# The products with V of a batch in two groups of two quads on TensorE, in place of three groups

## The chip, the core and the metric

The kernel runs on one NeuronCore of a Trainium2 chip. The metric is the device time of one execution in microseconds, as the median of several runs; the profile comes from one profiled execution, whose own time stands beside its span below.

## The reference

A block of a transformer: cross-attention over a context with a mask, and a mixture of experts behind it. Cut to what matters here:

```
q = split_heads(layernorm(x) @ Wq.T + bq)      # 16 batches, 112 rows, 16 heads of 16
k = split_heads(ctx @ Wk.T + bk)               # 16 batches, 375 rows
v = split_heads(ctx @ Wv.T + bv)
scores = einsum('bhqd,bhkd->bhqk', q, k) / 4
p = softmax(where(mask == 0, -1e9, scores))
x = x + einsum('bhqk,bhkd->bhqd', p, v) @ Wo.T + bo
# then: layernorm, a router, the top 2 of 8 experts for each row, x = x + their weighted sum
```

## The kernel before

Everything is float32 or a split of a float32 number into two parts (a high and a low one), so that a projection is three products. The 16 batches are worked on one after the other in a software pipeline. The function turn(b) of TensorE (L1653 to L1712) writes out by hand the order of the pipeline's turn b, for b = 0 to 14. In a turn TensorE does four things for four different batches, and VectorE (DVE) and ScalarE (ACT) run their own turns, also in an order written out by hand; the engines meet only through semaphores. Nothing is reordered by a scheduler: each engine takes its instructions in the order of the code.

The names that are used from here on, all of them for TensorE work in turn b:

- **H0 to H15** (L1539, heads): scores of one head of the next batch, b+1, 112 x 376, one matmul each. They are only for the row maxima: DVE reads each of them from its bank of PSUM (L1053, "neg_max") to find the maximum. There are two banks for 16 heads, so head s waits until DVE has read head s-2.
- **V0, V2, V1** (values): the values of batch b+1, six matmuls each at L1478.
- **K00, K01, K10, K11** (keys): the keys of batch b+3, in four parts of three matmuls at L1478. In turns 13 and 14 there is no such batch; the output projections of finished rows stand in place of K01 and K11 (12 matmuls each), and K00 and K10 are empty.
- **S0 to S3** (L1554, scores): scores of batch b for softmax, transposed, with mask and maxima folded in; one quad (four heads) each, six matmuls into three banks of PSUM. ACT takes the exponential of a quad in one instruction, L815, here exp0 to exp3, and writes it to one of two buffers ("probs"). All four quads use the same three banks, so each S waits for the exp of the quad before it.
- **O0 to O3** (L1568, outputs): the products with V of the quad. Four heads stand side by side in strips of 32 columns of the array (a tile_position at L1570), 12 matmuls and 12 weight loads of 32 columns, which the profile shows as 24 of each. O(j) waits for exp(j); exp(j+2) waits for O(j), since it writes the same buffer.
- **OT**, **AT** (L1581, L1593): transposes of the finished attention rows of batch b-1. ACT reads AT (L808), then DVE (L1044, "attn_low").
- **MT** (L1544): the transpose of the 16 maxima of batch b+1, at the end of the turn, into the bank that the even heads use. DVE reads it in two instructions (L1062, L1064, here "max_rows") and two DMAs carry it to the operand of the next turn's S0.

Before a turn's first head, H0, TensorE waits for max_rows of the turn before, since H0 overwrites MT's bank; before H1 it waits for attn_low, since H1 overwrites AT's bank:

```
if s >= 2:
    pe.wait_ge(max_read, H * b.n + s - 1)
elif s == 0 and not early(b, 1):
    pe.wait_ge(mx_ready, 2 * b.n)
elif s == 1 and not early(b, 3):
    pe.wait_ge(tl_ready, KD * (b.n - 2))
```

DVE's own order in a turn is: the maxima of H0 to H10, a normalisation, the maxima of H11 to H13, the keys of K01, the maxima of H14 and H15, the keys of K11, max_rows, attn_low. In turn 14 the statistics of finished rows stand ahead of its first maximum. ACT's order around the four exps is: two casts, a copy of the outputs, a copy of values, exp0, a copy of values, exp1, exp2, the two instructions on AT, exp3.

After turn 14 the code for the last batch follows (L1871 on), which begins with O2 and O3 of batch 14, and then the router, a plan of the experts' steps, and the experts' steps.

Of the kernel before, what the change touches and what calls it, by code (L numbers as in the profile page):

```python
# [105 lines left out]
def xattn_moe_kernel(nc, x_rows, x_tiles, ctx_t, mask, wq_t, wk_t, wv_t, wo_t, bq, bk, bv, bo,  # L106
                     router_w, w1, w2, out):
    ctx = ExitStack()
    with ctx:
# [281 lines left out]
        def has(b):  # L391

            return not isinstance(b.n, int) or 0 <= b.n < B
# [1080 lines left out]
        def _(pe):  # L1474
# [6 lines left out]
            def project_keys(b, t, halves=range(KD)):  # L1481
                home = ctx_home(b.n)
                if 0 not in halves:
                    pass
                elif t == 0:
                    pe.wait_ge(ch_ready, b.n + 1)
                    pe.wait_ge(cl_ready, b.n + 1)

                    if early(b, 4):
                        if b.n:  # L1490
                            pe.wait_ge(*{1: (vx_ready, 2), 2: (kf_ready, 4), 3: (vx_ready, 4)}[b.n])
                    else:
                        pe.wait_ge(vx_ready, 2 * (b.n - 1))
                elif not early(b, 4):
                    pe.wait_ge(an_ready, b.n - 3)
                m = slice(t * P, (t + 1) * P)
                terms = [(w[:, 0, k, m], c[home][:, k, :]) for k in halves for w, c in ((wh, ch), (wl, ch), (wh, cl))]
                last = product(ps[:, BK_KV + t, 0:CP], terms, first=0 in halves, final=KD - 1 in halves)
                if KD - 1 in halves:
                    last.then_inc(kproj_done, 1)  # L1500

            def project_values(b, k3):

                if early(b, 1):
                    pe.wait_ge(kf_ready, 2)
                elif k3 == 0:
                    if has(b.after(1)):
                        pe.wait_ge(kf_ready, 2 * b.n + 3)
                    else:
                        pe.wait_ge(resid_added, 1)  # L1510
                elif k3 == 2:
                    if has(b.after(1)):
                        pe.wait_ge(kf_ready, 2 * b.n + 4)
                    else:
                        pe.wait_ge(resid_added, 2)
                m = slice(k3 * CT, (k3 + 1) * CT)
                last = product(ps[0:CT, BK_KV + k3 // 2, D * (k3 % 2):D * (k3 % 2) + D],
                               [(c[ctx_home(b.n)][:, k, m], w[:, 2, k, :]) for k in range(KD)
                                for w, c in ((wh, ch), (wh, cl), (wl, ch))])
                if k3 != 0:  # L1520
                    last.then_inc(vproj_done, 1)
# [3 lines left out]
            def head_scores(b, turns):  # L1525

                for s in turns:
                    if s == 0:
                        pe.wait_ge(q_stacked[b.ring], 48 * (b.lap + 1))
                        pe.wait_ge(k_stacked[b.ring], 96 * (b.lap + 1))  # L1530
# [7 lines that stand above are left out]
                    a, q = s % 2, s // 2  # L1538
                    pe.matmul(ps[0:S, BK_MAX + a, 0:CP], qs[b.ring][0:R_MAX, q, S * a:S * (a + 1)],  # L1539
                              ks[b.ring][0:R_MAX, q, :], start=True, stop=True).then_inc(smax_done, 1)  # L1540

            def max_transpose(b):
                pe.wait_ge(max_read, H * (b.n + 1))
                pe.transpose(ps[0:H, BK_MAX, 0:S], neg_max[:, :], ident[0:S, 0:S]).then_inc(maxt_done, 1)  # L1544

            def quad_scores(b, j):

                if j == 0:
                    pe.wait_ge(mx_stacked[b.ring], 32 * (b.lap + 1))
                if not (early(b, 1) and j < 1):  # L1550
                    pe.wait_ge(pf_ready, QUADS * b.n + j)
                for k3 in range(KT):
                    for q in range(2):
                        last = pe.matmul(ps[0:CT, BK_ST + k3, 2 * S * q:2 * S * (q + 1)],  # L1554
                                         ks[b.ring][0:ROWS, 2 * j + q, k3 * CT:(k3 + 1) * CT],
                                         qs[b.ring][0:ROWS, 2 * j + q, :], start=True, stop=True)
                last.then_inc(st_done, 1)

            def quad_outputs(b, j):

                pe.wait_ge(pf_ready, QUADS * b.n + j + 1)
                if j == 0:
                    pe.wait_ge(vx_ready, 2 * (b.n + 1))
                    if not early(b, 1):
                        pe.wait_ge(ot_ready, b.n)
                for k3 in range(KT):
                    for i in range(4):
                        last = pe.matmul(ps[VC * i:VC * (i + 1), BK_OUT, S * j:S * (j + 1)],  # L1568
                                         vx[b.par][:, k3, 2 * j + i // 2 + HALF * (i % 2), :], pf[j % 2][:, k3, S * i:S * (i + 1)],
                                         start=k3 == 0, stop=k3 == KT - 1, tile_position=(0, VC * i))  # L1570
                last.then_inc(pv_done, 1)

            def out_transpose(b):
                pe.wait_ge(ot_ready, b.n + 1)

                if has(b.after(2)):
                    pe.wait_ge(vx_ready, 2 * b.n + 5)
                else:
                    pe.wait_ge(resid_added, 4 if has(b.after(1)) else 6)
                for j in range(QUADS):  # L1580
                    last = pe.transpose(ps[0:S, BK_KV + 1, P * j:P * (j + 1)], ot[:, S * j:S * (j + 1)], ident[:, :])  # L1581
                last.then_inc(ott_done, 1)
# [70 lines left out]
            def turn(b):  # L1653

                after, before = b.after(1), b.after(-1)

                def heads(*numbers):
                    if has(after):
                        head_scores(after, numbers)

                def scores(j):
                    if has(b):
                        quad_scores(b, j)

                def outputs(of, j):
                    if has(of):
                        quad_outputs(of, j)

                def values(k3):
                    if has(after):  # L1670
                        project_values(after, k3)

                def keys(t, *halves):
                    if has(b.after(3)):
                        project_keys(b.after(3), t, halves)
                    elif halves[-1] == KD - 1:
                        project_output(2 * (b.n - B + 3) + t)

                outputs(before, 2)
                heads(0)  # L1680
                values(0)
                heads(1, 2)
                outputs(before, 3)
                heads(3)
                values(2)
                heads(4, 5)
                scores(0)
                heads(6)
                if has(before):
                    out_transpose(before)  # L1690
                heads(7)
                values(1)
                heads(8, 9)
                scores(1)
                heads(10)
                outputs(b, 0)
                heads(11)
                keys(0, 0)
                heads(12)
                scores(2)  # L1700
                heads(13)
                keys(0, 1)
                heads(14)
                keys(1, 0)
                heads(15)
                keys(1, 1)
                scores(3)
                if has(after):
                    max_transpose(after)
                if has(before):  # L1710
                    attn_transpose(before)
                outputs(b, 1)  # L1712

            first = Batch(0, 0)

# [46 lines left out]
            for b in range(B - 1):  # L1762
                turn(Batch(0, b))
# [108 lines left out]
            before = last.after(-1)  # L1872
# [92 lines left out]
```

## Time and profile before

| what | value |
|---|---|
| time, median of 3 runs | 485.5 us (484.94 to 486.68) |
| time of the profiled execution | 485.71 us |
| span in the profile of that execution | 483.9 us |
| mean granted TensorE clock | 0.929 of full speed |
| busy: TensorE matmul, VectorE, ScalarE | 417.6, 346.5, 268.5 us |

In the profile's rows a time is in microseconds from the start of the span, and the second number is how long the row lasted. "PE" is TensorE's matmuls, "PEld" its weight loads. Matmuls overlap: each row shows a matmul from its start to the end of its way through the array, so the distance from one start to the next is what it costs. A matmul whose weight load could not be hidden shows a row that is some 0.09 us longer than others of its kind (0.43 against 0.34 us for a head, 0.91 against 0.81 us for a quad of scores), because the row then begins with the load. Where starts are subtracted below, such a row counts from 0.09 or 0.10 us later, and that is called its effective start.

### The profile page before, as it was taken

What the parts mean: (1) busy time and instruction counts of PE and PEld (TensorE: products, weight loads), DVE (VectorE), ACT (ScalarE), POOL (GpSimd) and SP (SyncE); (2) the same over time, 40 slices, a digit from 0 to 9 for tenths busy, and PEclk for the clock granted to TensorE, in tenths of its full rate; (3) what the DMA queues carried; (4) which work ended last, traced back from release to release, by engine and by line L of the source; (5) the groups of instructions that cost most, each with busy time, mean ns of one, the idle gap of its engine ahead of it and who ended that gap; (6) DMA issues with size and microseconds to landing.
All of it is one profiled execution on the core that took longest, in us unless ns stands there. A gap on an engine that the chain in (4) does not pass through costs nothing.

```text
span 483.9 us, 10747 instructions
## 1 busy us (share of the span) xinstructions
PE 417.6 (86%) x4187; PEld 387.0 (80%) x4187; DVE 346.5 (72%) x711; ACT 268.5 (55%) x351; POOL 227.4 (47%) x255
## 2 busy tenths in 40 slices
PE   1584669999999999999999999677999999999820
PEld 1472559999999999999999888577999999999820
DVE  2685557787788887787878868874787777767536
ACT  3322225666666556666655464515887888888600
POOL 7263334422322343332220365647477888875430
PEclk9796878999999999999999999659999999999975
DMA  7868947766768887866745027943122322332159
GB/s 170 214 158 180 285 159 160 160 130 145 163 150 163 155 183 152 177 146 135 147 94 108 2 91 260 364 143 93 56 87 78 88 88 88 88 87 78 45 195 303
DMA packets 60227, 69.83 MB, mean 144 GB/s; under 512 B 19185, under 2 KB 55298, under 8 KB 60178
## 3 DMA queue, kind: packets, MB, share of 16 engines
q1 hardware_dynamic: 54242, 56.30, 48.3%
q0 software_dynamic: 4032, 11.02, 7.7%
q10 hardware_dynamic: 1904, 1.84, 1.1%
q8 instruction: 33, 0.54, 0.5%
q14 instruction: 16, 0.13, 0.1%
HBM read 35.64 MB, written 14.78 MB: 104 GB/s over the span
## 4 chain that ended last, share of the span: by engine, by line
PE 73%; DVE 10%; issue 6%; DMA 5%; ACT 2%; POOL 2%; SPq 0%; POOLq 0%; DVEq 0%; ACTq 0%
PE ps L1478 37%; PE ps L1539 12%; PE ps L1554 9%; PE ps L1568 8%; PE ps L1833 2%; PE ps L1581 1%; DVE x_rows_sb L1100 1%; DVE neg_max L1053 1%; DMA y_rows<-y_out,slot_of_row 1%; DMA y_back<-y_rows 1%; DMA rows<-xn_rows,token_of_row 1%; DVE stats L1089 1%; POOL rows L746 1%; DMA keep<-keep_scratch 1%; DMA q_stack<-max_rows 1%
## 5 line engine op out<-in xcount | busy, mean ns | idle before, releaser
L1053 DVE TENSOR_REDUCE neg_max<-ps 112x1 f32<-112x376 f32 x256 | 133.7, 546 | 38.5 <-PE ps L1539 33.7
L815 ACT ACTIVATE probs<-ps 125x1344 f32<-125x1344 f32 x64 | 82.8, 1293 | 43.3 <-PE ps L1554 38.1
L1539 PE MATMUL ps<-k_stack,q_stack 98*112 98x376 f32 x256 | 88.7, 381 | 10.2 <-issue 5.9
L587 POOL TENSOR_TENSOR k_lo<-k_f,k_hi 128x752 fp32r<-128x752 f32 x16 | 28.9, 1804 | 121.9 <-ACT k_hi L789 119.5
L1539 PEld LDWEIGHTS ps<-k_stack,q_stack 98*112 98x112 f32 x256 | 45.7, 181 | 23.6 <-DVE neg_max L1053 13.7
L746 POOL DMA_INDIRECT rows<-xn_rows,token_of_row x42 | 55.2, 1315 | 19.0 <-issue 12.5
L754 POOL DMA_INDIRECT y_rows<-y_out,slot_of_row x42 | 46.4, 1104 | 27.5 <-ACT y_out L985 16.5
L1554 PE MATMUL ps<-q_stack,k_stack 100*125 100x224 f32 x384 | 53.3, 275 | 0.2 <-DMA q_stack<-max_rows 0.2
L1554 PEld LDWEIGHTS ps<-q_stack,k_stack 100*125 100x125 f32 x384 | 51.2, 191 | 1.1 <-ACT probs L815 0.5
L1478 PE MATMUL ps<-w_hi,h_hi 128*128 128x256 f32 x168 | 48.6, 289 | 1.6 <-issue 1.6
L1478 PE MATMUL ps<-flat_t_hi,w_hi 128*128 128x256 f32 x168 | 47.6, 283 | 1.3 <-DVE flat_t_lo L1365 1.3
L1478 PE MATMUL ps<-flat_t_hi,w_lo 128*128 128x256 f32 x168 | 47.3, 282 | 0.0
L1478 PE MATMUL ps<-flat_t_lo,w_hi 128*128 128x256 f32 x168 | 47.3, 282 | 0.0
L1478 PE MATMUL ps<-w_hi,h_lo 128*128 128x256 f32 x168 | 47.0, 280 | 0.0
L1568 PE MATMUL ps<-probs,v_wide 125*32 125x112 f32 x1536 | 47.0, 262 | 0.0
L1478 PE MATMUL ps<-w_lo,h_hi 128*128 128x256 f32 x168 | 46.9, 279 | 0.0
L1568 PEld LDWEIGHTS ps<-probs,v_wide 125*32 125x32 f32 x1536 | 35.1, 109 | 8.0 <-issue 5.6
L966 ACT ACTIVATE h_f<-ps 128x1024 f32<-128x1024 f32 x21 | 21.5, 1026 | 25.2 <-PE ps L1478 25.2
L1478 PEld LDWEIGHTS ps<-flat_t_hi,w_hi 128*128 128x128 f32 x168 | 32.1, 191 | 1.7 <-DVE flat_t_lo L1365 1.7
L1478 PEld LDWEIGHTS ps<-w_hi,h_hi 128*128 128x128 f32 x168 | 31.9, 190 | 2.0 <-issue 1.8
L1387 DVE TENSOR_TENSOR h_lo<-h_f,h_hi 128x1024 fp32r<-128x1024 f32 x21 | 25.7, 1225 | 10.1 <-ACT h_hi L971 10.1
L1478 PE MATMUL ps<-ctx_hi,attn_w_hi 128*128 128x376 f32 x64 | 23.2, 363 | 10.5 <-POOL ctx_lo L578 9.7
(202 smaller groups left out, 1032.4 us busy)
## 6 DMA issues: line engine op xcount, KB each, us to landing
k_stack<-k_hi SPq DMA_DIRECT2D x64, 188.0 KB, 4.5
w_all<-w SPq DMA_DIRECT2D x2, 4096.0 KB, 18.2
k_stack<-k_lo SPq DMA_DIRECT2D x32, 188.0 KB, 5.5
ctx_raw<-ctx_t SPq DMA_DIRECT2D x32, 187.5 KB, 5.4
q_stack<-q_scratch SPq DMA_DIRECT2D x32, 168.0 KB
q_scratch<-q_hi SPq DMA_DIRECT2D x16, 224.0 KB, 3.0
y_back<-y_rows SPq DMA_DIRECT2D x14, 256.0 KB, 4.5
q_scratch<-q_lo SPq DMA_DIRECT2D x8, 224.0 KB, 2.9
```

The lines of the kernel that those rows point to most:

```text
L587: pool.tensor_tensor(kl[:, :, :], kf[:, :, :], kh[:, :, :].bitcast(F32), ALU.subtract)\
L746: pool.indirect_dma_start(rows[t.ring][:, a, :], None, xn_rows, row_of(token_i, t, a))\
L754: pool.indirect_dma_start(y_rows, row_of(slot_i, t, a), yo[t.par][:, a, :], None)\
L815: act.activation(pf[j % 2][:, :, :], ps[0:CT, BK_ST:BK_ST + KT, 0:4 * S], ACT.Exp).then_inc(pf_ready, 1)
L966: act.activation(hf[t.par][:, :, :], silu_source(t), ACT.Silu).then_inc(hf_ready, 1)
L1053: dve.tensor_reduce(neg_max[:, s:s + 1], ps[0:S, BK_MAX + s % 2, 0:CP], AX.X, ALU.max, negate=True).then_inc(max_read, 1)
L1387: dve.tensor_tensor(hl[t.par][:, :, :], hf[t.par][:, :, :], hh[t.par][:, :, :].bitcast(F32), ALU.subtract).then_inc(hl_ready, 1)
L1478: last = pe.matmul(o, lhs, rhs, start=first and n == 0, stop=final and n == len(terms) - 1)
L1539: pe.matmul(ps[0:S, BK_MAX + a, 0:CP], qs[b.ring][0:R_MAX, q, S * a:S * (a + 1)], ks[b.ring][0:R_MAX, q, :], start=True, stop=True).then_i ...
L1554: last = pe.matmul(ps[0:CT, BK_ST + k3, 2 * S * q:2 * S * (q + 1)], ks[b.ring][0:ROWS, 2 * j + q, k3 * CT:(k3 + 1) * CT], qs[b.ring][0:ROW ...
L1568: last = pe.matmul(ps[VC * i:VC * (i + 1), BK_OUT, S * j:S * (j + 1)], vx[b.par][:, k3, 2 * j + i // 2 + HALF * (i % 2), :], pf[j % 2][:, ...
L1833: last = pe.transpose(ps[:, BK_T + t.par, TG * k + P * a:TG * k + P * (a + 1)], rows[t.ring][:, a, k * P:(k + 1) * P], ident[:, :])
```

## The change

The four quads of outputs that are done in a turn stood in three places: O2 of the batch before at the turn's start, right behind O1 at the end of the turn before (one group of two), O3 behind H2, and O0 between H10 and H11. Now O2 stands beside O3 behind H2, and O0 and O1 stand together behind S2. The same instructions are issued, in another order, on TensorE alone.

```diff
@@ -1676,10 +1676,10 @@
-                outputs(before, 2)
                 heads(0)
                 values(0)
                 heads(1, 2)
+                outputs(before, 2)
                 outputs(before, 3)
                 heads(3)
                 values(2)
@@ -1692,12 +1692,12 @@
                 values(1)
                 heads(8, 9)
                 scores(1)
-                heads(10)
-                outputs(b, 0)
-                heads(11)
+                heads(10, 11)
                 keys(0, 0)
                 heads(12)
                 scores(2)
+                outputs(b, 0)
+                outputs(b, 1)
                 heads(13)
                 keys(0, 1)
                 heads(14)
@@ -1709,7 +1709,6 @@
                     max_transpose(after)
                 if has(before):
                     attn_transpose(before)
-                outputs(b, 1)
```

TensorE's instructions across the boundary between two turns, before: MT, AT, O1 and O2 (x12 each), H0, the six matmuls of V0, then H1 and H2.

```order
L1544 MATMUL ps<-ident,neg_max 16x112
L1593 MATMUL ps<-ident,attn_rows 128x112 x2
L1568 MATMUL ps<-probs_97,v_wide_94 32x112 x12
L1568 MATMUL ps<-probs_96,v_wide_94 32x112 x12
L1539 MATMUL ps<-k_stack_90,q_stack_92 112x376
L1478 MATMUL ps<-attn_w_hi,ctx_hi_115 125x256
L1478 MATMUL ps<-attn_w_hi,ctx_lo_116 125x256
L1478 MATMUL ps<-attn_w_lo,ctx_hi_115 125x256
L1478 MATMUL ps<-attn_w_hi,ctx_hi_115 125x256
L1478 MATMUL ps<-attn_w_hi,ctx_lo_116 125x256
L1478 MATMUL ps<-attn_w_lo,ctx_hi_115 125x256
L1539 MATMUL ps<-k_stack_90,q_stack_92 112x376 x2
```

The same boundary on TensorE now; O2 and O3 follow after H1 and H2.

```order
L1544 MATMUL ps<-ident,neg_max 16x112
L1593 MATMUL ps<-ident,attn_rows 128x112 x2
L1539 MATMUL ps<-k_stack_90,q_stack_92 112x376
L1478 MATMUL ps<-attn_w_hi,ctx_hi_115 125x256
L1478 MATMUL ps<-attn_w_hi,ctx_lo_116 125x256
L1478 MATMUL ps<-attn_w_lo,ctx_hi_115 125x256
L1478 MATMUL ps<-attn_w_hi,ctx_hi_115 125x256
L1478 MATMUL ps<-attn_w_hi,ctx_lo_116 125x256
L1478 MATMUL ps<-attn_w_lo,ctx_hi_115 125x256
L1539 MATMUL ps<-k_stack_90,q_stack_92 112x376 x2
L1568 MATMUL ps<-probs_96,v_wide_94 32x112 x12
L1568 MATMUL ps<-probs_97,v_wide_94 32x112 x12
```

Between MT with AT and H0 two quads of outputs have gone; nothing stands there now.

The middle of a turn on TensorE before, from S1: H10, O0, H11, K00 (three matmuls), H12, S2, H13.

```order
L1554 MATMUL ps<-q_stack_93,k_stack_91 125x224 x6
L1539 MATMUL ps<-k_stack_113,q_stack_114 112x376
L1568 MATMUL ps<-probs_96,v_wide_94 32x112 x12
L1539 MATMUL ps<-k_stack_113,q_stack_114 112x376
L1478 MATMUL ps<-ctx_hi_84,attn_w_hi 128x376
L1478 MATMUL ps<-ctx_hi_84,attn_w_lo 128x376
L1478 MATMUL ps<-ctx_lo_86,attn_w_hi 128x376
L1539 MATMUL ps<-k_stack_113,q_stack_114 112x376
L1554 MATMUL ps<-q_stack_93,k_stack_91 125x224 x6
L1539 MATMUL ps<-k_stack_113,q_stack_114 112x376
```

The same stretch of TensorE now, from S1: H10 and H11 in one row, K00, H12, S2, O0, O1, H13.

```order
L1554 MATMUL ps<-q_stack_93,k_stack_91 125x224 x6
L1539 MATMUL ps<-k_stack_113,q_stack_114 112x376 x2
L1478 MATMUL ps<-ctx_hi_84,attn_w_hi 128x376
L1478 MATMUL ps<-ctx_hi_84,attn_w_lo 128x376
L1478 MATMUL ps<-ctx_lo_86,attn_w_hi 128x376
L1539 MATMUL ps<-k_stack_113,q_stack_114 112x376
L1554 MATMUL ps<-q_stack_93,k_stack_91 125x224 x6
L1568 MATMUL ps<-probs_96,v_wide_94 32x112 x12
L1568 MATMUL ps<-probs_97,v_wide_94 32x112 x12
L1539 MATMUL ps<-k_stack_113,q_stack_114 112x376
```

Between S1 and S2 a quad of outputs has gone, and behind S2 two have come.

## Rows read from the trace of the kernel before

**Rows 1.** The page, part 4: the chain that ended last, share by engine.

```profile
PE 73%; DVE 10%; issue 6%; DMA 5%; ACT 2%; POOL 2%; SPq 0%; POOLq 0%; DVEq 0%; ACTq 0%
```

**Rows 2.** Waits of PE's matmuls, 66 to 280 us: total, times, longest.

```profile
PE ps L1539 <- DVE neg_max L1053: 2.3, 2, 1.9
```

**Rows 3.** Windows: stretch, its length, busy of engines, granted clock (PEclk), DMA share.

```profile
65.00:79.00 14.00, 11.92 (x54) 11.10 (x54) 7.43 (x17) 5.64 (x8) 7.88 (x11) 0.70 0.57 158
...
208.00:222.00 14.00, 14.00 (x177) 12.75 (x175) 11.30 (x26) 8.62 (x11) 4.82 (x3) 1.00 0.66 141
```

**Rows 4.** Timeline of PE (start, length, line): MT ending turns 1 and 12.

```profile
97.86 0.26 PE L1544 MATMUL ps<-ident,neg_max 112*16 112x112 f32 x1
...
249.07 0.26 PE L1544 MATMUL ps<-ident,neg_max 112*16 112x112 f32 x1
```

**Rows 5.** Timeline of PE, one boundary: MT, O1+O2, H0, H1+H2, O3, H3.

```profile
207.90 0.26 PE L1544 MATMUL ps<-ident,neg_max 112*16 112x112 f32 x1
...
208.28 1.36 PE L1568 MATMUL ps<-probs,v_wide 125*32 125x112 f32 x48
...
209.56 0.43 PE L1539 MATMUL ps<-k_stack,q_stack 98*112 98x376 f32 x1
...
210.54 0.51 PE L1539 MATMUL ps<-k_stack,q_stack 98*112 98x376 f32 x2
...
210.99 0.78 PE L1568 MATMUL ps<-probs,v_wide 125*32 125x112 f32 x24
...
211.70 0.43 PE L1539 MATMUL ps<-k_stack,q_stack 98*112 98x376 f32 x1
```

**Rows 6.** Timeline of DVE and ACT there: max_rows, attn_low, exp3, maximum of H0.

```profile
208.49 0.26 DVE L1064 TENSOR_TENSOR max_rows<-ps,max_rows 16x112 fp32r<-16x112 f32 x1
209.02 0.58 DVE L1044 SCALAR_TENSOR_TENSOR attn_t_lo<-ps,bv_c,attn_t_hi 128x112 fp32r<-128x112 f32 x2 [0.27 <-ACT attn_t_hi L808]
209.19 1.29 ACT L815 ACTIVATE probs<-ps 125x1344 f32<-125x1344 f32 x1 [0.20 <-PE ps L1568]
...
210.03 0.55 DVE L1053 TENSOR_REDUCE neg_max<-ps 112x1 f32<-112x376 f32 x1 [0.43 <-PE ps L1539]
```

**Rows 7.** Timeline of PE, the middle of that turn: O0, S2, H13.

```profile
202.84 0.78 PE L1568 MATMUL ps<-probs,v_wide 125*32 125x112 f32 x24
...
204.50 0.82 PE L1554 MATMUL ps<-q_stack,k_stack 100*125 100x224 f32 x6
...
205.16 0.34 PE L1539 MATMUL ps<-k_stack,q_stack 98*112 98x376 f32 x1
```

**Rows 8.** Timeline of DVE and ACT there: maxima of H8 to H10, exp1.

```profile
201.88 1.62 DVE L1053 TENSOR_REDUCE neg_max<-ps 112x1 f32<-112x376 f32 x3 [0.33 <-PE ps L1539]
...
202.72 1.29 ACT L815 ACTIVATE probs<-ps 125x1344 f32<-125x1344 f32 x1 [0.43 <-PE ps L1554]
```

**Rows 9.** Timeline of ACT and PE in turn 13: exp1, S2, H13.

```profile
257.64 1.29 ACT L815 ACTIVATE probs<-ps 125x1344 f32<-125x1344 f32 x1 [0.42 <-PE ps L1554]
...
258.98 0.91 PE L1554 MATMUL ps<-q_stack,k_stack 100*125 100x224 f32 x6
259.74 0.33 PE L1539 MATMUL ps<-k_stack,q_stack 98*112 98x376 f32 x1
```

**Rows 10.** Timeline, turn 14's start: exp3, maxima of H0 to H2, H2, O3.

```profile
265.06 1.29 ACT L815 ACTIVATE probs<-ps 125x1344 f32<-125x1344 f32 x1 [0.20 <-PE ps L1568]
...
266.53 1.61 DVE L1053 TENSOR_REDUCE neg_max<-ps 112x1 f32<-112x376 f32 x3
...
267.13 0.42 PE L1539 MATMUL ps<-k_stack,q_stack 98*112 98x376 f32 x1 [0.38 <-DVE neg_max L1053]
267.48 0.78 PE L1568 MATMUL ps<-probs,v_wide 125*32 125x112 f32 x24
```

**Rows 11.** Timeline of PE behind turn 14: S0 of the last batch, O3.

```profile
283.04 0.92 PE L1554 MATMUL ps<-q_stack,k_stack 100*125 100x224 f32 x6 [0.21 <-DMA q_stack<-max_rows]
283.88 0.78 PE L1568 MATMUL ps<-probs,v_wide 125*32 125x112 f32 x24
```

## The prediction, made before the changed kernel ran

> **What bounds the kernel now.** I read the chain of work that ended last first: 73% of it is PE, 10% DVE [rows 1]. So the question is whether PE has gaps in the stretch that changes, the 15 turns. It has nearly none: the list of waits shows 2.3 us for heads that waited for DVE's maxima, in two cases [rows 2], and the window of a whole turn shows PE's matmuls busy for 14.00 of 14 us while DVE has 11.30 and ACT 8.62, with the granted clock at 1.00 [rows 3]. The turns are alike: MT starts at 97.86 at the end of turn 1 and at 249.07 at the end of turn 12, eleven turns of 13.75 us [rows 4]. A turn of DVE is thus 81% full, and every one of its 16 maxima is tied to a head on PE by two banks. PE is full because the order by hand puts other work wherever a head or a quad of scores would have to wait. The change takes such work out of two places, so I ask at each what would then be late.
>
> **What the change saves.** Nothing is computed less. A group of outputs costs something on the way in and on the way out. Way in: H2 starts 0.17 us after H1 (210.71), and O3 at 210.99, 0.28 us after H2 where a head takes 0.17: 0.11 us [rows 5]. The quad's 24 weight loads fill 0.54 us of the row; from O3's start to H3's effective start (211.79) it is 0.80, so 0.26 us on the way out [rows 5]. That is 0.37 us for a group. Over the turns 44 groups become 30 (behind turn 14, O2 keeps a group of its own), so 14 x 0.37 = 5.2 us, if nothing is late next. The row shows this cost; beside it, the Trainium skill (TensorEngine Tiling (Array Packing), Tiling Modes, Key Properties) says that a change of tiling mode drains the array, which speaks for the change, and the trace agrees with its 0.11 and 0.26 us.
>
> **What is late next, first place: the middle of a turn.** S2 needs exp1, and exp1 needs S1. Before, O0 lay between S1 and S2 and hid part of that exp. exp1 runs from 202.72 to 204.01, while S2 started at 204.50 [rows 7, 8], so before it waited for nothing. How soon S2 can follow an exp is seen in turn 13, where it did wait: exp1 ended at 258.93, S2's effective start is 259.08, a release of 0.15 us [rows 9]. With O0 gone from there, S2 can start at 204.01 + 0.15 = 204.16, 0.34 us earlier than before, not the 0.91 us (0.37 of the group and 0.54 of its loads) that left. The heads are not later than that: the maximum of H9 ends two thirds into the row of three, at 202.96, of H10 at 203.50 [rows 8]; with a release of 0.14 us (next part) H11 starts at 203.10, three matmuls of K00 of 0.17 bring H12 to 203.78, S2 could start at 203.95. ACT decides.
> Behind S2 now stand two quads. From the effective start of a quad of scores to the outputs behind it: 283.15 to 283.88, 0.73 us [rows 11]. From the start of a double group to the effective start of the head behind it: 208.28 to 209.65, 1.37 us [rows 5]. So H13 comes at 204.16 + 0.73 + 1.37 = 206.26, where it was 205.16: **1.10 us later**. From H13 on the order is the same to MT. exp2 now waits for O0 too, whose row would run from 204.89 to 205.67; with 1.29 us it is over by 207.0, and S3, which waits for it, stands right ahead of MT, now at 209.0: hidden. I take 1.10 for turns 0 to 12, 14.3 us. In turns 13 and 14 K00 is empty and S2 waited for exp1 already [rows 9]; its start stays, and H13 comes 0.73 + 1.37 - 0.66 = 1.44 us later, 2.9 us for the two.
>
> **Second place: the boundary of two turns.** Before, MT to H3 took 207.90 to 211.79, 3.89 us, with three quads in it [rows 5]; now it has two. H0 needs max_rows, which ended at 208.75 [rows 6], 0.9 us before H0's effective start of 209.65; O1 and O2 covered it. They are gone. The release from DVE to PE is seen where a head did wait: the first of three maxima ended at 266.53 + 0.54 = 267.07, H2's effective start was 267.21, 0.14 us [rows 10]. So H0 starts at 208.89, where it could have followed AT at about 208.28. H1 follows 0.89 us behind, as before, at 209.78; attn_low, which it needs too, ends at 209.60 [rows 6], with its release at 209.74: just hidden, and 0.1 us dearer if V0 ran faster. DVE reads H0 when attn_low is over, 209.60, for 0.55 us, ending between 210.06 (such rows overlap by up to 0.09) and 210.15; H2 starts at 210.20 to 210.29, where 0.17 behind H1 would be 209.95. I take 210.22. O2 begins 0.28 later at 210.50, H3 at 210.50 + 1.37 = 211.87: **0.1 us later** than before, though a quad less was done. O3 needs exp3, which before ended at 210.48 [rows 6] and cannot be later now; O3's turn is at 211.06: hidden. Twelve boundaries at 0.1 give 1.2 us; the one behind turn 0 has no attn_low, I take 0. In front of H2 of turn 14 DVE decides already (it waited 0.38 us) [rows 10]; its start stays, two quads follow in place of one, 1.37 - 0.80 = 0.57 us.
> This rests on V0 and O2 not passing H0 while it waits. In turn 14 exp3 was over at 266.35, and O3 still started only after H2 had waited until 267.13 [rows 10]. That is a rule against this change in the Trainium skill (TensorE: Matmul & The Clock Gate, Part 3, what overlaps and what doesn't): matmuls start and end in program order, only weight loads are pulled ahead; the trace agrees, and if it didn't, H0's wait would be filled.
>
> **The end.** Behind turn 14, O1 no longer stands ahead of S0 of the last batch. S0 waited there for the DMA of max_rows (0.21 us) [rows 11], so the missing 0.57 us come back as a longer wait: 0. DVE, ACT, POOL and the DMA queues get the same instructions in the same order, and longer turns give the loads more room. All that follows hangs on the attention's last rows, so the delay goes through to the end.
>
> **The sum.** 14.3 + 2.9 + 1.2 + 0.6 = 19.0 us on the profiled execution's 485.7 (span 483.9 and 1.8 around it); that execution is 0.2 above the median, so 485.5 + 19.0 = 504.5 us. Read as parts of a turn: 0.37 us saved, some 1.5 us of new waits. Bounds: the release behind an exp or a maximum between 0 (as if hidden) and twice what the rows show moves S2, H0 and H2 by 0.15 each, at most some 0.3 us a turn, 4.5 us over 15 turns; the way into a double group behind S2 between the 0.73 us of rows 11 and 0.1 more adds 1.5 above; the end between 0 and the -0.57 that its cover is worth. That makes 499 to 510.5.
>
> **The rivals.**
> *Fewer groups, waits hidden*: the 5.2 us saved come through, 480.3 us, faster. For it: PE is full, DVE and ACT have 2.7 and 5.4 us to spare in the 14 us. It decides on whether the new waits stay under 0.37 us a turn. Against it: H0 alone waits about 0.6 us for max_rows, whose rows lie on a chain through DVE that nothing shortens. 4%; exactly cancelled, 485.5 us, 2%.
> *Only one place costs*: if H0 hardly waits (max_rows done earlier, since DVE's keys end earlier against MT), the boundary gains about 0.6 us a turn instead of losing 0.1, 13 x 0.7 = 9 us less: 495 us. Against it: from H13 to MT the order is unchanged on every engine, so max_rows should end 0.85 us behind MT's start as before [rows 5, 6]. 10%.
> *The clock*: the stretch from 65 to 79 us shows a granted clock of 0.70 with PE busy for only 11.92 of 14 us, among the waits of 1.9 us for DVE [rows 2, 3]. If waits that are now some 1.5 us of a 15 us turn cost one tenth of the clock over the loop, PE's 13.5 us become 15.0, 1.5 us for 15 turns, 22 us more: 527 us. Between, 511 to 527, if it strikes a part of the turns. Against it: in the rows the clock is at 1.00 in turns with waits of 0.38 us, and the longest new one is about 0.6. The Trainium skill (TensorE: Matmul & The Clock Gate, Part 1) says that an idle array falls to half its clock; no row here shows it for gaps this short. 7%.
> *The forecast*, new waits in both places: 77%.
>
> **How the numbers follow.** The forecast's 504.5 is the likeliest. About 0.3% is what a measurement of this kernel can tell from no change, so faster is 0.04, within 0.3% 0.02, slower 0.94. For 8 in 10, the forecast's bounds and the near part of the two neighbours: 498 to 510.5.
>
> **What would show it.** Right: MT to MT near 15.0 us instead of 13.75; H13 some 2.1 us behind S2's start; PE idle before H0 ended by max_rows, before H2 ended by a maximum, before S2 ended by exp1; 29 double groups and no single ones before the end of turn 14; the same busy time of DVE and ACT over a longer span. Wrong: a turn of 13.4 us with H0 right behind AT (then the waits are hidden), a turn near 14.3 us with an idle time before S2 alone (one place), or a granted clock under 1.00 between 85 and 280 us.

## The result: 503.75 us, slower by 3.9%

The changed kernel takes 503.75 us (median of 4 runs, 502.56 to 505.8) against 485.48 us for the kernel before (4 runs); the ratio is 1.0386, with a 95% interval of 1.0349 to 1.0422. The forecast was 504.5 us, in a range of 498 to 510.5. The profiled execution, the slowest of the four, took 505.8 us with a span of 504.0.

The profile page's chain of work that ended last, by engine, beside [rows 1]; then the list of waits of PE's matmuls and of its weight loads, of 66 to 300 us (total, times, longest), beside [rows 2]; then two lines of the same list for the kernel before:

```profile
PE 66%; DVE 16%; issue 6%; DMA 5%; ACT 3%; POOL 2%; SPq 1%; POOLq 0%; DVEq 0%; ACTq 0%
```

```profile
PE ps L1539 <- DVE max_rows L1064: 7.9, 14, 0.7
PE ps L1539 <- DVE neg_max L1053: 3.7, 4, 2.3
...
PEld ps L1554 <- ACT probs L815: 5.1, 15, 0.4
PEld ps L1568 <- issue: 2.5, 14, 0.2
```

```profile
PEld ps L1568 <- issue: 5.6, 31, 0.2
...
PEld ps L1554 <- ACT probs L815: 0.5, 2, 0.2
```

PE's share of the chain fell from 73% to 66%, DVE's rose from 10% to 16%. One wait is new in the list of matmuls: 14 times before H0 for max_rows, 0.56 us each. Among the weight loads the wait of S2 for exp1, which stood there twice before (turns 13 and 14), now stands there 15 times, 0.34 us each. The idle time on the way into a group of outputs, 5.6 us in 31 places before, is 2.5 us in 14. This list is not a count of groups: PE's timeline has 29 double groups up to the end of turn 14, as forecast, and only those behind H2 show such an idle time. So there are fewer groups, and PE now waits where the quads stood. A whole turn in a window (stretch, length, busy of PE, PEld, DVE, ACT, POOL, granted clock, DMA) and the MTs at the ends of turns 1 and 12, beside [rows 3, 4]:

```profile
219.00:233.00 14.00, 13.41 (x168) 11.74 (x168) 9.95 (x23) 8.58 (x11) 4.82 (x3) 1.00 0.67 141
```

```profile
99.84 0.26 PE L1544 MATMUL ps<-ident,neg_max 112*16 112x112 f32 x1
...
263.82 0.26 PE L1544 MATMUL ps<-ident,neg_max 112*16 112x112 f32 x1
```

PE is busy for 13.41 of 14 us in place of 14.00, at the full clock. Eleven turns take 163.98 us, 14.91 us each where it was 13.75: 1.16 us more a turn.

The boundary of two turns, timeline of PE and of DVE (start, length): MT, H0, H1 and H2, O2 and O3, H3; then max_rows, attn_low, the maximum of H0; beside [rows 5, 6]:

```profile
219.15 0.26 PE L1544 MATMUL ps<-ident,neg_max 112*16 112x112 f32 x1
...
220.15 0.40 PE L1539 MATMUL ps<-k_stack,q_stack 98*112 98x376 f32 x1 [0.55 <-DVE max_rows L1064]
...
221.10 0.68 PE L1539 MATMUL ps<-k_stack,q_stack 98*112 98x376 f32 x2
...
221.71 1.36 PE L1568 MATMUL ps<-probs,v_wide 125*32 125x112 f32 x48
...
223.00 0.42 PE L1539 MATMUL ps<-k_stack,q_stack 98*112 98x376 f32 x1
```

```profile
219.75 0.26 DVE L1064 TENSOR_TENSOR max_rows<-ps,max_rows 16x112 fp32r<-16x112 f32 x1
...
220.28 0.58 DVE L1044 SCALAR_TENSOR_TENSOR attn_t_lo<-ps,bv_c,attn_t_hi 128x112 fp32r<-128x112 f32 x2 [0.27 <-ACT attn_t_hi L808]
...
220.77 0.54 DVE L1053 TENSOR_REDUCE neg_max<-ps 112x1 f32<-112x376 f32 x1
```

H0's effective start is 220.21 (its row is 0.06 us longer than the plain 0.34), 1.06 us after MT, behind max_rows, which ended at 220.01. H3's effective start is 223.08, 3.93 us behind MT: as long as before (3.89 us) with two quads in it in place of three.

The middle of the next turn, the same way: exp1 on ACT, then PE's S2, O0 and O1, and H13; beside [rows 7, 8]:

```profile
227.75 1.29 ACT L815 ACTIVATE probs<-ps 125x1344 f32<-125x1344 f32 x1 [0.42 <-PE ps L1554]
...
229.10 0.91 PE L1554 MATMUL ps<-q_stack,k_stack 100*125 100x224 f32 x6
...
229.94 1.36 PE L1568 MATMUL ps<-probs,v_wide 125*32 125x112 f32 x48
...
231.23 0.43 PE L1539 MATMUL ps<-k_stack,q_stack 98*112 98x376 f32 x1
```

exp1 ends at 229.04, S2's effective start is 229.20, H13 follows at 231.32. From H3 to the next MT (234.07) it is now 10.99 us, where it was 9.83 (211.79 to 221.62): 1.16 us more with one quad more.

### The profile page after: what moved, and what is told of

It reads as the page before. It is cut to its first block, busy times and chain, and to the rows that moved or that the text cites. A ratio compares the mean times of both kernels' runs of the same rounds, so it can differ in the third digit from the quotient of the medians.

```text
span 504.0 us, 10747 instructions
## 1 busy us (share of the span) xinstructions
PE 428.4 (85%) x4187; PEld 390.4 (77%) x4187; DVE 344.3 (68%) x711; ACT 268.0 (53%) x351; POOL 227.5 (45%) x255
## 4 chain that ended last, share of the span: by engine, by line
PE 66%; DVE 16%; issue 6%; DMA 5%; ACT 3%; POOL 2%; SPq 1%; POOLq 0%; DVEq 0%; ACTq 0%
PE ps L1478 33%; PE ps L1539 11%; PE ps L1568 8%; PE ps L1554 8%; DVE neg_max L1053 4%; DVE k_f L1037 3%; PE ps L1832 2%; PE ps L1581 1%; DMA y_back<-y_rows 1%; DMA y_rows<-y_out,slot_of_row 1%; DVE x_rows_sb L1100 1%; DMA rows<-xn_rows,token_of_row 1%; ACT probs L815 1%; DVE max_rows L1064 1%; DVE max_rows L1062 1%
## 5 line engine op out<-in xcount | busy, mean ns | idle before, releaser
L1539 PE MATMUL ps<-k_stack,q_stack 98*112 98x376 f32 x256 | 92.7, 392 | 19.6 <-DVE max_rows L1064 7.9
L1554 PE MATMUL ps<-q_stack,k_stack 100*125 100x224 f32 x384 | 54.6, 278 | 0.8 <-DMA q_stack<-max_rows 0.4
L1568 PE MATMUL ps<-probs,v_wide 125*32 125x112 f32 x1536 | 44.1, 261 | 0.0
L1478 PEld LDWEIGHTS ps<-flat_t_hi,w_lo 128*128 128x128 f32 x168 | 32.7, 194 | 0.0
## 6 DMA issues: line engine op xcount, KB each, us to landing
w_all<-w SPq DMA_DIRECT2D x2, 4096.0 KB, 18.3
```

What stands on the lines that cost most here:

```text
L1478: last = pe.matmul(o, lhs, rhs, start=first and n == 0, stop=final and n == len(terms) - 1)
```

## Experiments

Two theories stood against each other. **Two separate waits**: in the middle O0 was the cover of exp1, at the boundary O1 and O2 were the cover of max_rows and attn_low, and the groups saved are worth less than that. **Only one of the places costs**, or only the number of groups counts. Seven kernels take the change apart, and the changed kernel ran once more beside three of them. In the table a turn is the distance of the MTs at the ends of turns 1 and 12, divided by 11.

| run | median, us | of the kernel before beside it | ratio, 95% interval | a turn, us |
|---|---|---|---|---|
| before | 485.5 | | | 13.75 |
| after | 503.75 | 485.48 | 1.0386 (1.0349 to 1.0422) | 14.91 |
| again | 503.13 | 485.23 | 1.0369 (1.0334 to 1.0403) | 14.91 |
| mid | 495.64 | 485.2 | 1.0237 (1.0184 to 1.029) | 14.35 |
| o0 | 493.7 | 485.2 | 1.019 (1.0141 to 1.0238) | 14.30 |
| bnd | 487.08 | 485.2 | 1.0042 (1.0014 to 1.0069) | 13.82 |
| split | 490.01 | 485.2 | 1.0095 (1.0045 to 1.0145) | 14.09 |
| v0 | 504.2 | 485.23 | 1.0362 (1.0316 to 1.0408) | 14.90 |
| ahead | 498.29 | 485.23 | 1.0269 (1.023 to 1.0307) | 14.66 |
| ahead2 | 497.04 | 485.23 | 1.0223 (1.0155 to 1.0291) | 14.36 |

**One quad alone (o0).** From the kernel before:

```diff
-                heads(10)
-                outputs(b, 0)
-                heads(11)
+                heads(10, 11)
                 keys(0, 0)
                 heads(12)
                 scores(2)
+                outputs(b, 0)
```

> One quad alone is moved: O0 from between H10 and H11 to behind S2, the rest as before. As many groups as before. The theory: S2 then waits for exp1 uncovered; from S2's effective start to H13 0.73 + 0.80 us, so H13 comes at 204.16 + 1.53 = 205.69 in place of 205.16 in the turn of the trace, 0.53 us later in 13 turns and 0.87 us in two: 485.5 + 8.6 = 494.1 us, with PE waiting 0.3 us before S2 for exp1 and 0.3 us before H11 for a maximum. If the order in the middle is indifferent as long as the groups are as many: 485.5 us.

493.7 us, 0.55 us more a turn. The timeline of PE in its middle, S2, O0, H13:

```profile
220.74 0.91 PE L1554 MATMUL ps<-q_stack,k_stack 100*125 100x224 f32 x6
...
221.58 0.78 PE L1568 MATMUL ps<-probs,v_wide 125*32 125x112 f32 x24
...
222.30 0.42 PE L1539 MATMUL ps<-k_stack,q_stack 98*112 98x376 f32 x1
```

S2's row is 0.91 us long, as it is after a wait, and H13 follows S2's effective start (220.84) by 1.54 us; 1.53 was expected. No quad has crossed a boundary and no group was added or lost: this is the price of taking O0 from between S1 and S2. O0 covered two waits there, that of S2 for exp1 and that of H11 for DVE's maximum of H9; ahead and ahead2 below tell them apart.

**The middle alone (mid).** As o0, and O1 follows O0 behind S2 instead of standing at the turn's end; O2 stays at the turn's start.

> The change in the middle of a turn alone: O0 and O1 stand together behind S2, O2 stays at the turn's start, O3 behind H2. As many groups of outputs as before (44). The theory of two separate waits: S2 is bound by exp1, H13 comes 1.10 us later in turns 0 to 12 and 1.44 us in turns 13 and 14 (17.2 us); at the boundary O2 alone still covers max_rows, so the boundary is about 0.47 us shorter by O1 that has left it, 13 times (6.1 us): 485.5 + 11.1 = 496.6 us. If only the number of groups counted: 485.5 us. If the boundary were what costs: near 485 to 487 us.

495.64 us, 0.60 us more a turn (0.63 by the terms of the expectation). Timeline of PE at a boundary: MT, O2, H0, H3.

```profile
212.72 0.26 PE L1544 MATMUL ps<-ident,neg_max 112*16 112x112 f32 x1
...
213.11 0.78 PE L1568 MATMUL ps<-probs,v_wide 125*32 125x112 f32 x24
213.82 0.43 PE L1539 MATMUL ps<-k_stack,q_stack 98*112 98x376 f32 x1
...
216.00 0.42 PE L1539 MATMUL ps<-k_stack,q_stack 98*112 98x376 f32 x1
```

O2 alone covers max_rows: H0 starts right behind it, and MT to H3 is 3.36 us, 0.53 less than before.

**The boundary alone (bnd).** From the kernel before; O1 stays at the turn's end:

```diff
-                outputs(before, 2)
                 heads(0)
                 values(0)
                 heads(1, 2)
+                outputs(before, 2)
                 outputs(before, 3)
```

> The change at the boundary alone, by half: O2 moves to O3 behind H2, O1 stays at the turn's end and O0 between H10 and H11. As many groups as before (44). The theory: O1 alone covers nearly all of max_rows' wait; H2 is about 0.1 us late, a boundary costs 0.1 us, the one into turn 14 0.57 us: 485.5 + 1.8 = 487.3 us, PE idle before H0 near zero. If moving O2 to O3 were itself the cost (a longer group that delays exp or the copy of the outputs): half of the loss and more, 494 us or above. If only the number of groups counted: 485.5 us.

487.08 us, 0.07 us more a turn: within a microsecond of the expectation. MT to H3, again by PE's timeline, is 3.94 us (207.38 to 211.32):

```profile
207.38 0.26 PE L1544 MATMUL ps<-ident,neg_max 112*16 112x112 f32 x1
...
207.76 0.78 PE L1568 MATMUL ps<-probs,v_wide 125*32 125x112 f32 x24
208.47 0.43 PE L1539 MATMUL ps<-k_stack,q_stack 98*112 98x376 f32 x1
...
211.23 0.43 PE L1539 MATMUL ps<-k_stack,q_stack 98*112 98x376 f32 x1
```

mid and bnd each hold a part of the change; together they are the whole. A turn of mid is 0.60 us longer, one of bnd 0.07, but one of after 1.16: 0.49 us more than the sum. That is, within 0.04 us, the 0.53 us by which mid's boundary got shorter. One quad covers the wait for max_rows as well as two; it appears in full when the second leaves too.

**The price of a group (split).** The kernel before with O3 in two parts around H3. The function takes the thirds of a quad as an argument for this; of the edit, only the lines of the order are shown:

```diff
-                outputs(before, 3)
+                outputs(before, 3, range(2))
                 heads(3)
+                outputs(before, 3, range(2, KT))
```

> The price of a group by itself: the kernel before with O3 cut in two around H3 (8 matmuls ahead of H3, 4 behind), which adds one group in 14 turns and moves nothing else. By the rows of before a group costs 0.11 us on the way in and 0.26 on the way out: 14 x 0.37 = 5.2 us, 490.7 us. If the ways in and out are hidden by the weight loads ahead: 485.5 us. If they cost more than the rows show, above 492 us.

490.01 us; 0.34 us a turn, 0.37 was taken from the rows of before. So a group has this price here: 4.8 us for 14 groups more. That the groups that the change saves have the same price at their own places is not shown by itself.

**V0 as cover of H0 (v0).** From the changed kernel:

```diff
-                heads(0)
                 values(0)
-                heads(1, 2)
+                heads(0, 1, 2)
```

> The changed kernel with V0 ahead of H0 at each turn's start, so that 0.7 us of other work covers the wait for max_rows. The theory that a second wait stands right behind: H0 starts at about the same time as before it (max_rows ends then), H1 follows at 0.17 us but now waits for attn_low, and H2 waits for DVE to read H0 behind attn_low, so H2 and all after it come no earlier: 503.8 us (within 1.5), the idle time in front of H0 moved to H1 and H2. If the wait of 0.55 us in front of H0 is what the boundary costs: 13 x 0.55 = 7 us less, 496.6 us.

504.2 us, a turn of 14.90: nothing gained. The list of waits and the timeline of PE (MT, H0, H1 and H2, O2 and O3, H3):

```profile
PE ps L1539 <- DVE attn_t_lo L1044: 4.6, 13, 0.4
```

```profile
219.30 0.26 PE L1544 MATMUL ps<-ident,neg_max 112*16 112x112 f32 x1
...
220.32 0.38 PE L1539 MATMUL ps<-k_stack,q_stack 98*112 98x376 f32 x1
221.06 0.88 PE L1539 MATMUL ps<-k_stack,q_stack 98*112 98x376 f32 x2 [0.36 <-DVE attn_t_lo L1044]
221.87 1.36 PE L1568 MATMUL ps<-probs,v_wide 125*32 125x112 f32 x48
223.15 0.42 PE L1539 MATMUL ps<-k_stack,q_stack 98*112 98x376 f32 x1
```

max_rows has left the list, and attn_low stands in it, 13 times 0.35 us in front of H1. MT to H3 is 3.93 us as in after. Three links of DVE stand in a row there, max_rows, attn_low and the maximum of H0; work of 0.7 us ahead of the first only moves the wait to the next.

**Filling the middle's wait (ahead, ahead2).** From the changed kernel, the group of O0 and O1 ahead of S2 in place of behind it:

```diff
-                scores(2)
                 outputs(b, 0)
                 outputs(b, 1)
+                scores(2)
```

> The changed kernel with the group of O0 and O1 ahead of S2 in place of behind it, behind H12, so that it fills PE's wait for exp1. By the rows of after: O0 could begin at 229.04, S2 at 230.41, H13 at 231.07 in place of 231.32, 0.25 us less in each of 15 turns: 500.0 us, PE's wait for exp1 gone and the one in front of H11 left. If S2's wait is not on the path: 503.8 us. If a later S2 makes exp2 and with it S3 late: above 504 us.

498.29 us; the turn is 0.25 us shorter, as expected, and turns 13 and 14 by 0.35 each. Expected were 500.0 us; 11 turns by 0.25 and the four others by some 0.3 make 4 us, and the medians differ by 4.8 from again, inside the intervals. Timeline of PE, H10 and H11, H12, O0 and O1, S2, H13:

```profile
223.85 0.85 PE L1539 MATMUL ps<-k_stack,q_stack 98*112 98x376 f32 x2
...
225.05 0.34 PE L1539 MATMUL ps<-k_stack,q_stack 98*112 98x376 f32 x1
225.32 1.36 PE L1568 MATMUL ps<-probs,v_wide 125*32 125x112 f32 x48
226.61 0.92 PE L1554 MATMUL ps<-q_stack,k_stack 100*125 100x224 f32 x6
227.36 0.34 PE L1539 MATMUL ps<-k_stack,q_stack 98*112 98x376 f32 x1
```

H12 to H13 takes 2.31 us, in after 2.56 (228.76 to 231.32). H10 and H11 still take 0.85 us, as in after, where two heads without a wait take 0.51: H11 waits for DVE's maximum of H9, for which PE's weight loads stand idle for 0.28 us. And with K00 between H10 and H11, and the group between H11 and H12:

```diff
-                heads(10, 11)
+                heads(10)
                 keys(0, 0)
+                heads(11)
+                outputs(b, 0)
+                outputs(b, 1)
                 heads(12)
                 scores(2)
-                outputs(b, 0)
-                outputs(b, 1)
```

> The changed kernel with K00 between H10 and H11 and the group of O0 and O1 between H11 and H12, ahead of S2, so that both waits of the middle are filled (H11's for the maximum of H9, S2's for exp1). By the rows of after: H11 at 228.33, O0 at 228.61, O1 when exp1 is over, H12 at 229.98, S2 230.15, H13 at 230.81 in place of 231.32, 0.51 us less in 15 turns: 7.6 us, 496.1 us, still slower than before by the boundary. If the middle's cost is the two quads themselves and not waits: 503.8 us.

497.04 us and a turn of 14.36, 0.55 us shorter than after (0.51 was expected). So filling the wait for exp1 alone gives 0.25 us a turn, since H11's wait for the maximum of H9 is left, and filling both gives 0.55. What is left against the kernel before, 0.61 us a turn, is more than the boundary's own 0.04 (MT to H3 is 3.93 us here too). The rest is 0.57 us, which is what a second quad adds to a group (1.37 - 0.80 us): it still stands in the middle and not where it had been cover at no cost.

The changed kernel beside them:

> The changed kernel again, to stand beside the three runs that change it: 503.8 us (502.6 to 505.8 so far).

503.13 us. An order of two groups that beats the kernel before was not found: the orders that fill the waits here are all slower than it, and others were not tried.

## Why the prediction was right

**The saving.** 0.37 us for a group was worked out from two distances of one boundary; split measures 0.34. The 0.03 us lie in the way out: it was taken against 0.54 us of weight loads, but a second quad lengthens a group by 0.57 us in the same rows, and 0.11 + 0.80 - 0.57 = 0.34. The forecast's sum does not use the 0.37; it adds distances that hold the groups as they stand.

**The middle.** S2's release behind exp1 was taken as 0.15 us from turn 13 and is 0.16 (229.04 to 229.20). From S2 to H13 the sum 0.73 + 1.37 = 2.10 us came out as 2.12. That gave 1.10 us a turn; the stretch from H3 to MT shows 1.16. Half of this difference lies in those two, the rest is not assigned. That S2's start is set by exp1, with the heads 0.2 us ahead of it, fits ahead and ahead2: the wait for exp1 alone gives back 0.25 us.

**The boundary.** H0 was expected 0.99 us behind MT and came at 1.06, since its release behind max_rows is 0.20 us and not 0.14. This error does not reach H3, since H2 waits for DVE's maximum of H0, which DVE takes behind attn_low: H2 starts 2.29 us behind MT (221.44) where 2.32 was taken, and DVE begins to read H0 0.09 us before attn_low's row ends. MT to H3 was forecast at 3.97 us and is 3.93, in before 3.89. That the second wait stands right behind the first, on which this part rests, v0 shows by itself.

**Turns 13 and 14, and the end.** Here the forecast said 1.44 us in the middle for each, and 0.57 at the boundary into turn 14, where DVE's statistics decide H2's start. The MTs of turns 12 to 14 and S0 behind turn 14, in PE's timeline:

```profile
280.03 0.26 PE L1544 MATMUL ps<-ident,neg_max 112*16 112x112 f32 x1
...
283.39 0.42 PE L1539 MATMUL ps<-k_stack,q_stack 98*112 98x376 f32 x1 [1.09 <-DVE neg_max L1053]
...
297.38 0.26 PE L1544 MATMUL ps<-ident,neg_max 112*16 112x112 f32 x1
...
300.96 0.92 PE L1554 MATMUL ps<-q_stack,k_stack 100*125 100x224 f32 x6 [0.42 <-DMA q_stack<-max_rows]
```

Turn 13 takes 16.21 us, 1.51 more than before (14.70); turn 14 takes 17.35, 2.04 more (15.31); 1.54 and 2.01 were expected. H2 of turn 14 starts 3.36 us behind MT in both kernels, now after a wait of 1.09 us. At the end S0 is 3.58 us behind MT, before 3.96: 0.4 us are won back, where 0 was taken. It still waits for the DMA of max_rows (0.42 us, before 0.21); the chain of work shows 2.41 us for that DMA and 2.78 in the kernel before, so what came back is the DMA's and not the quad's. In again the same kernel has 2.09 us for the DMA and S0 3.27 us behind MT: it differs from execution to execution.

**The sum.** 11 turns by 1.16, turn 1 by 1.2, 1.5 and 2.0 for the last two, and -0.4 at the end make 17.1 us, where the forecast, without its 1.1 for turn 0, has 17.9. Turn 0 is between 1.2 us (again) and 2.1 us (after) longer, but this can't be told from what differs ahead of it: MT at its end comes 0.8 us later than before in after and 0.6 us earlier in again. From S0 to the end of the span after takes 2.2 us more than before and again 1.2, which the forecast did not have and no run explains. The medians differ by 18.3; 19.0 were forecast. So the turns carry the agreement; that some unexplained microsecond outside them brings the total nearer to the forecast is luck.

**The rivals.** All four kernels with fewer groups (after, v0, ahead, ahead2) are slower than the kernel before. One place alone: this rival needed H0 to wait hardly at all, and it waits 0.56 us. mid and bnd show that the boundary by itself costs 1.9 us and the middle 10.4, but the whole (17.9 to 18.3) is some 6 us above their sum, so both places take part. The clock of after stayed at 1.00 from 98 to 297 us, in two windows:

```profile
98.00:264.00 166.00, 159.49 (x1919) 140.84 (x1918) 121.28 (x269) 94.62 (x122) 48.10 (x29) 1.00 0.68 140
264.00:297.40 33.40, 30.61 (x371) 26.84 (x370) 24.21 (x59) 15.02 (x19) 7.92 (x12) 1.00 0.26 49
```

The prediction's argument that the clock holds in a turn with a wait of 0.38 us had no row beside it; the trace of before bears it out, with 1.00 from 264 to 279 us. Its other argument, that the longest new wait is about 0.6 us, is wrong: the wait before H2 of turn 14 grew from 0.38 to 1.09 us. The clock held behind it here and fell behind it in one other run (below).

## What to carry to other kernels

In a hand-made order, ask of each block of work not what it costs where it stands, but whose latency it covers: here one quad between S1 and S2 hid an exponential and a maximum, and moving it behind S2 cost 0.55 us a turn, as much as its weight loads fill. A cover of two blocks can hide that each alone would do; the loss comes with the last one, so parts of a change that look free one at a time need not be free together. Before filling a new wait, look which wait stands right behind it on the same engine: when three links of DVE follow each other, covering the first gained nothing.

## What the runs showed of the hardware that was not expected

The granted clock fell behind a wait of about 1 us in one trace, and did not in four others. In the profiled execution of ahead2, H2 of turn 14 waits for DVE as it does in after, with the same busy time around it, and then the clock falls. Windows around that wait, of after and of ahead2 (stretch, length, busy of PE and the others, granted clock, DMA), and the rows of H2 and of O2 and O3 in ahead2:

```profile
282.00:283.40 1.40, 0.31 (x4) 0.04 (x2) 1.33 (x7) 0.30 (x1) 0.38 (x1) 1.00 0.03 5
283.40:285.00 1.60, 1.60 (x49) 1.28 (x49) 0.94 (x2) 0.00 (x0) 1.49 (x2) 1.00 0.00 0
```

```profile
274.10:275.50 1.40, 0.32 (x4) 0.05 (x2) 1.33 (x7) 0.30 (x1) 0.38 (x1) 1.00 0.03 5
275.50:276.50 1.00, 1.00 (x13) 0.68 (x17) 0.72 (x2) 0.00 (x0) 0.89 (x2) 0.52 0.00 0
276.50:278.40 1.90, 1.90 (x44) 1.63 (x36) 0.22 (x1) 0.00 (x0) 1.90 (x2) 0.50 0.00 0
```

```profile
275.49 0.65 PE L1539 MATMUL ps<-k_stack,q_stack 98*112 98x376 f32 x1 [1.08 <-DVE neg_max L1053]
276.06 2.47 PE L1568 MATMUL ps<-probs,v_wide 125*32 125x112 f32 x48
```

In both, PE was busy for 0.3 of 1.40 us ahead of it. In after the clock stays at 1.00; in ahead2 it stands at 0.52 and 0.50, the lower of its two levels (1.2 of 2.4 GHz), for some 3 us, and the group of O2 and O3 there lasts 2.47 us in place of 1.36. Turn 14 of that execution takes 18.31 us, 0.96 more than in after, although its other turns are 0.55 us shorter. In the traces of again, ahead and v0 H2 of turn 14 waits for about as long (1.08, 1.08 and 1.18 us), and the clock stays at 1.00 behind it. What decides is not shown. Four runs of ahead2 spread from 492.93 to 499.44 us; whether this clock is the reason was not tested.
